# Row maxima sent apart from the reciprocal sums, and a scan 21 groups ahead instead of 24, in a fused attention and binary-convolution kernel

## What is computed

```python
f = jnp.einsum('kc,bcn->bkn', w1, xf) + b1[None, :, None]      # 16 features
energy = jnp.einsum('bkn,bkm->bnm', f, f)
attention = jax.nn.softmax(energy, axis=-1)
out = jnp.einsum('bcm,bnm->bcn', xf, attention)
x = x + out * 0.1
...
y = conv(sign(x), alpha * sign(w)); y = batch_norm(y) * gamma + beta; return y + x
```

## Time and profile before

| | us |
|---|---|
| median of 3 runs (1984.22 to 1986.18) | 1985.28 |
| profiled execution | 1984.29 |
| its span, first to last instruction | 1982.5 |
| first attention matmul starts | 60.74 |
| last `P` of attention starts | 1756.28 |
| busy: PE, DVE, ACT, POOL | 1908.3, 1567.9, 1420.2, 1211.2 |

### The profile page before, as it was taken

One profiled execution on the slowest core, in us unless ns is written; L12 is line 12 of the kernel. 1 busy time (PEld: TensorE's weight loads), 2 busy tenths in 40 slices (PEclk: granted clock), 3 DMA queues, 4 the chain that ended last, 5 costly groups with the idle time before them and its releaser, 6 DMA issues. The chain is left out here.

```text
span 1982.5 us, 40003 instructions
## 1 busy us (share of the span) xinstructions
PE 1908.3 (96%) x15232; PEld 1638.3 (83%) x15232; DVE 1567.9 (79%) x2151; ACT 1420.2 (72%) x2793; POOL 1211.2 (61%) x848
## 2 busy tenths in 40 slices
PE   7999999999999999999999999999999999999990
PEld 2799999998998899998999999988998999864440
DVE  5777787788877877788877777788887887767787
ACT  5777777777777777778777777778777777652335
POOL 4556555667855555567755556677665556468760
PEclk6899999999999999999999999999999999999995
DMA  6111111012211111012111110112111102434009
GB/s 213 41 51 60 53 39 35 32 64 64 69 46 59 61 40 32 32 68 95 58 56 62 40 31 25 56 54 63 32 32 32 32 30 77 156 120 162 1 39 385
DMA packets 58287, 133.67 MB, mean 67 GB/s; under 512 B 9328, under 2 KB 9328, under 8 KB 57584
## 3 DMA queue, kind: packets, MB, share of 16 engines
q1 hardware_dynamic: 58096, 131.10, 19.4%
HBM read 84.48 MB, written 33.62 MB: 60 GB/s over the span
## 5 line engine op out<-in xcount | busy, mean ns | idle before, releaser
L760 POOL CAST Ph<-P 128x1024 fp32r<-128x1024 f32 x496 | 725.9, 1464 | 625.2 <-ACT P L518 625.2
L610 DVE TENSOR_REDUCE nb<-scw 128x1 f32<-128x512 f32 (+1 forms) x988 | 680.9, 690 | 288.6 <-PE scw L408 283.6
L529 ACT ACTIVATE scw<-scw,nb 128x512 f32<-128x512 f32 (+1 forms) x988 | 655.7, 664 | 317.6 <-DVE nb L610 317.3
L426 PE MATMUL accb<-Ph,xh 64*128 64x512 f32 x2048 | 807.6, 394 | 1.3 <-ACT tb L539 1.3
L426 PE MATMUL acct<-Ph,xh 64*128 64x512 f32 x2048 | 804.9, 393 | 0.0
L426 PE MATMUL accb<-Ph,xl 64*128 64x512 f32 x2048 | 800.7, 391 | 0.0
L426 PE MATMUL acct<-Ph,xl 64*128 64x512 f32 x2048 | 796.8, 389 | 0.0
L620 DVE TENSOR_TENSOR Pl<-P,Ph 128x1024 fp32r<-128x1024 f32 x512 | 664.4, 1298 | 27.3 <-ACT Ph L523 15.9
L426 PE MATMUL acct<-Pl,xh 64*128 64x512 f32 x2048 | 635.7, 390 | 0.0
L426 PE MATMUL accb<-Pl,xh 64*128 64x512 f32 x2048 | 632.2, 388 | 0.0
L518 ACT ACTIVATE P<-ee 128x1024 f32<-128x1024 f32 x512 | 526.1, 1028 | 82.2 <-PE ee L399 66.1
(11 more groups left out here) (166 smaller groups left out, 1390.9 us busy)
## 6 DMA issues: line engine op xcount, KB each, us to landing
wk<-xt SPq DMA_DIRECT2D x32, 512.0 KB, 3.8
xres<-x SPq DMA_DIRECT2D x32, 512.0 KB, 3.8
x<-xres SPq DMA_DIRECT2D x32, 512.0 KB, 2.8
R<-rd SPq DMA_DIRECT2D x32, 256.0 KB, 3.1
xn<-x SPq DMA_DIRECT2D x16, 512.0 KB, 12.6
xr<-x SPq DMA_DIRECT2D x16, 512.0 KB, 10.5
out<-xr SPq DMA_DIRECT2D x16, 512.0 KB, 10.1
An<-x SPq DMA_DIRECT2D x14, 512.0 KB, 5.2
```

The costliest lines, as they stand in the source:

```text
L426: return pe.matmul(to[:, :], w[rows, g * GM + k, c * 128:(c + 1) * 128], p[rows, s, k * QC:(k + 1) * QC], start=g == 0 and i == 0, stop=g ...
L529: nc.scalar.activation(to, to, ACT.Exp, bias=nb[:, t % 2, w:w + 1], accum_out=bsum[:, t % 2, w:w + 1]).then_inc(bsum_done, 1)
L610: nc.vector.tensor_reduce(nb[:, t % 2, w:w + 1], of, AX.X, ALU.max, negate=True).then_inc(nmax_done, 1)
L760: nc.gpsimd.tensor_copy(Ph[:, e % RP, :], P[:, e % 2, :]).then_inc(ph_done, 1)
```

## The change

LAG becomes 21, so that 19 wide scans stand in the head instead of 22, and the last scan of chunk t + 1 falls in step 10 of chunk t instead of 7. The row chain is cut in two. `row_max` now also copies the maxima to `sr` and transposes them, all in step 10, and `shift_rows` sends these rows alone in step 11. The differences, weights, sum and reciprocal move into the chunk itself: `row_diff` in step 6, the exponential on ACT in 7, `row_weights` in 8, `row_sum` in 9, with tiles of their own (`inv`, `inv_t`) and a second transpose. SP sends them in step 10 (`inverse_rows`), before the maximum rows, and loads `R` in step 12 instead of 7; `scan_rows` goes from step 9 to 13. `part_groups` gets other steps for POOL's parts.

```diff
-LAG = 24
+LAG = 21
...
+        inv = sb("inv", [128, 32], F32)
+        inv_t = sb("inv_t", [128, 32], F32)
...
             if t % CH == 0:
-                return (2, 5, 6, 11, 12, 13)
+                return (2, 5, 11, 12, 13, 14)
             if t % CH == CH - 1:
-                return (1, 2, 4, 5, 11, 12)
-            return (1, 3, 5, 11, 12, 13)
+                return (1, 2, 4, 5, 12, 13)
+            return (1, 2, 4, 5, 12, 13)
...
+            def inverse_rows(t):
+                sp.wait_ge(turned, t + 1)
                 if t >= 1:
                     sp.wait_ge(r_in, 16 * t)
                 for j in range(4):
                     sp.dma_start(rd.rearrange("(i c) -> i c", i=QT)[:, j * 32:(j + 1) * 32],
-                                 rows_t[j * 32 + 2 * QT:j * 32 + 3 * QT, :]).then_inc(rd_out, 16)
+                                 inv_t[j * 32:j * 32 + QT, :]).then_inc(rd_out, 16)
...
-                    if g == 7 and t >= 0:
+                    if g == 10 and t >= 0:
+                        inverse_rows(t)
+                    if g == 12 and t >= 0:
                         load_r(t)
...
-                    if g == 9 and t + 3 < NT:
+                    if g == 13 and t + 3 < NT:
                         scan_rows(t + 3)
...
-                if g == 8 and 0 <= t + 1 < NT:
-                    act.wait_ge(dd_done, t + 2)
+                if g == 7 and t >= 0:
+                    act.wait_ge(dd_done, t + 1)
                     nc.scalar.activation(wg[:], dd[:], ACT.Exp).then_inc(wg_done, 1)
...
             def row_max(t):
                 dve.wait_ge(nmax_done, unit_count(SU * (t + 1) - 1))
                 if t > 0:
-                    dve.wait_ge(stat_done, t)
+                    dve.wait_ge(dd_done, t)
+                    dve.wait_ge(row_in, 64 * t)
                 nc.vector.tensor_reduce(negm[:], ...).then_inc(negm_done, 1)
                 dve.wait_ge(negm_done, t + 1)
                 nc.vector.tensor_copy(sh[:], negm[:]).then_inc(shift_h, 1)
+                dve.wait_ge(shift_h, t + 1)
+                nc.vector.tensor_copy(sr[:, 0:QT], sh[:].bitcast(F32))
+                nc.vector.tensor_tensor(sr[:, QT:2 * QT], negm[:], sh[:].bitcast(F32),
+                                        ALU.subtract).then_inc(stat_done, 1)
+                dve.wait_ge(stat_done, t + 1)
+                nc.vector.transpose(rows_t[:], sr[:]).then_inc(row_done, 1)
+
+            def row_diff(t):
+                if t > 0:
+                    dve.wait_ge(wg_done, t)
                 nc.vector.tensor_tensor(dd[:]..., ALU.subtract).then_inc(dd_done, 1)
...
             def row_weights(t):
...
-                if t > 0:
-                    dve.wait_ge(row_done, t)
-                dve.wait_ge(shift_h, t + 1)
-                nc.vector.tensor_copy(sr[:, 0:QT], sh[:].bitcast(F32))
-                nc.vector.tensor_tensor(sr[:, QT:2 * QT], negm[:], sh[:].bitcast(F32), ALU.subtract)
...
             def row_sum(t):
...
-                nc.vector.reciprocal(sr[:, 2 * QT:3 * QT], den[:]).then_inc(stat_done, 1)
-                dve.wait_ge(stat_done, t + 1)
+                nc.vector.reciprocal(inv[:, 0:QT], den[:]).then_inc(inv_done, 1)
+                dve.wait_ge(inv_done, t + 1)
                 if t > 0:
-                    dve.wait_ge(row_in, 64 * t)
                     dve.wait_ge(rd_out, 64 * t)
-                nc.vector.transpose(rows_t[:], sr[:]).then_inc(row_done, 1)
+                nc.vector.transpose(inv_t[:], inv[:]).then_inc(turned, 1)
...
-                if g == 7 and 0 <= t + 1 < NT:
+                if g == 2 * G - 1 - LAG and 0 <= t + 1 < NT:
                     row_max(t + 1)
-                if g == 9 and 0 <= t + 1 < NT:
-                    row_weights(t + 1)
-                if g == 10 and 0 <= t + 1 < NT:
-                    row_sum(t + 1)
+                if g == 6 and t >= 0:
+                    row_diff(t)
+                if g == 8 and t >= 0:
+                    row_weights(t)
+                if g == 9 and t >= 0:
+                    row_sum(t)
```

More of the change, by code:

```diff
@@ L171, in attention @@
         row_done = sem("row_done")
+        inv_done = sem("inv_done")
+        turned = sem("turned")
         rd_out = sem("rd_out")
@@ L701, in _ @@
             dve.wait_ge(col_in, 16)
-            dve.wait_ge(fill_done, 3)
+            dve.wait_ge(fill_done, 4)
             for t, g in steps:
@@ L743, in _ @@
             nc.gpsimd.memset(bsum[:], 0.0).then_inc(fill_done, 1)
+            nc.gpsimd.memset(inv[:], 0.0).then_inc(fill_done, 1)
             def lower_x(h):
```

## The result

The changed kernel takes 1989.66 us in the median of 15 runs (1986.82 to 1991.79), the kernel before, run beside it, 1985.65 (15 runs, 1984.22 to 1987.94). The ratio is 1.0019, 95% interval 1.0012 to 1.0026: 4.0 us slower, where no change was forecast. The median lies at the upper end of the range, 0.06 above its 1989.6; by the ratio, on the 1985.28 us from which the forecast was worked out, it would be 1989.05. The profiled execution took 1989.09 us, its span is 1987.3, against 1984.29 and 1982.5 before.

What follows compares the result with a forecast made beforehand. TensorE, busy 96% of the span, was taken as the bound. Terms 0 + 0 + 0 + 5.0 - 3.6 - 1.3 + 0 = +0.1 gave 1984.4 us profiled, 1985.4 as median (no change); range 1980.2 to 1989.6.

Steps and rivals of the forecast that it cites:

- The head: Before the first attention matmul: three fewer wide scans gain 0, as POOL's splitting of x holds it; ends -3.8 and +1.0 us.
- the prediction's own sign: In the head: forecast right if the first attention matmul comes within 0.5 us of 60.7, first energy matmul near 52.
- Rival C: At the first attention matmul: something besides POOL holds it, so 2.0 to 3.8 us come through, 1983.4 to 1981.6; chance 0.08.
- Scans moved into the steps: Six scans leave the head and run beside attention free, their maxima and sums in idle time: 0, ends 0 and +0.01.
- DVE's batch: Five row instructions in step 10: 0 in 26 normal chunks; POOL's split blocks one at image changes, 0.84 us six times, +5.0.
- Rival A: Step 10 at image changes: DVE's instructions slip past POOL unblocked, leaving -4.9 us, 1980.4; chance 0.20.
- rival B: Step 10 at image changes: the copy is blocked after the cast too, 1.5 us a chunk, +4.1, 1989.4; chance 0.12.
- POOL's parts: New steps for scaling, joining, adding at image changes: -3.6 us in first chunks, -1.3 in last chunks, together -4.9.
- The double that moved nearer the boundary: Image's last chunk: POOL step holding a part and a split of x, from 11 to 13; 0, ends -1.0, +1.5 a chunk.
- SP's queue: Transfers on SP: reciprocal rows first, then the row transfer, R loaded in step 12 and read in 15; all priced 0.
- Rival D: About 10 chunks behind disturbances: the array halves lie differently, 2.7 us either way, 1982.7 or 1988.1; chance 0.07.

## Why the prediction was right and wrong

- **The head, 0.** Right in its mechanism. The row transfer was issued at 49.59 behind the last piece of x. The first energy matmul came 0.5 us earlier (53.67), and between 52.2 and 54.2 in the experiments with this head, where 52.1 was worked out; the first attention matmul waited 1.59 us for `Ph`. It came at 61.63, which misses the prediction's own sign (within 0.5 us of 60.7) but lies inside the 2 us by which the head of the unchanged kernel scatters. Rival C is out, and the run with the casts on ACT shows why: the gain was there, in front of POOL.
- **Scans moved into the steps, 0.** This is the step that failed: "Their maxima and sums on DVE and ACT fall in steps where both have idle time" is true of chunk 13 (51.72) and false of chunk 30, where the weights' preparation fills those steps. It was missed because the prediction asked only TensorE about chunk 30, and never looked at what ACT and DVE do in steps 8 to 10 of that chunk. It measured +2.7, two thirds of the result, and the late weights took it away.
- **DVE's batch, 0 in 26 chunks, +5.0 in six.** The mechanism held: one instruction of the batch was blocked in each of the six, the cast in three and the copy in three. 0.88 in three chunks and 0.45 in three make 4.0; 0.84 was right for the last chunk of an image and twice too much for the first. That it fits the last is in part luck: the sum sets the idle 0.81 against the blocked time and the 0.52 behind it, but leaves out the maximum and the cast, 0.38, which stand in the same step. The traces suggest where the two sizes come from, though no run tests it: in chunk 7 DVE's next subtraction of P is held too, 1.87 us for 1.22, in chunk 8 it takes 1.38. Rival A is out, the batch did not slip through; so is rival B, no batch was blocked twice. Rival B's price was worked out otherwise than the forecast's own: with the 0.52 it would be 2.0 a chunk, about 1992.3, and beyond the range.
- **POOL's parts, -4.9.** Right in size: 1.10 in steps 9 and 10 of chunk 8 (forecast 1.2), and about 0.6 in steps 8 to 11 of chunk 7 (0.43), three times -1.7 is -5.1. For chunk 7 the cause was right too, the batch that leaves step 7. For chunk 8 it was wrong: the join in step 6 was given all of the 1.2, but the batch of the old step 7 suffices for it, so that the table alone is worth 0, and the right size is luck. The double that moved nearer the boundary was priced at 0 between -1.0 and +1.5: it cost 1.05 in step 0 and freed 1.05 in steps 14 and 15.
- **SP's queue, 0.** Right: PE's only wait for the rows in the whole trace is the one of 5.9 us in the head, and none for `R` appears.
- **Rival D, halves of the array.** Given 0.07, it happened in part: +2.1 in six chunks without a stall, 0.9 of it also between two executions of one kernel. The rest, 1.2, repeats in other kernels with this table and row chain, and its cause stays open.
- **The sum.** With the measured sizes: 4.0 - 5.1 + 2.7 + 2.1 + 0.4 + 0.7 = +4.8. The six disturbed chunks, on which nearly all of the working was spent, came within 1.2 us of the forecast; the loss came from two terms put at zero.

## What to carry to other kernels

When work moves by some steps, list for every engine what else stands in its new steps, in the special chunks too (first, last, image change); a window that shows one engine undisturbed says nothing of the others. A gain that ends in front of a busy engine can be stored and not lost: relieve that engine and measure again. Here six casts moved brought out 3.4 to 4.0 us with 21 groups and nothing with 24. And a stall with two sufficient causes shows no gain when either is removed alone, so try them together before dropping both.

## What the runs showed of the hardware that was not expected

- Which instruction of DVE's batch is blocked hangs on where POOL starts: in chunk 8 the cast of four elements took 1.30 us; in chunk 7 the cast passed with 0.22 us and the copy took 1.23; with the copy gone, the subtraction, both inputs in SBUF, took 1.21 instead of 0.15.
- A chunk with TensorE busy in every window takes 53.81 or 54.69 us in two executions of one kernel. How the two half-array streams come to lie so was not found.
- In the head one and the same program differs by 2 us in its first energy matmul. In the changed kernel's trace POOL waited 2.34 us for a piece of x at 37.69, which the trace of the kernel before does not have.
